# Two float32r parts in place of three bf16 parts in the last two mean passes

## What is computed

```
def _sage_layer(x, src, dst, W_l, b_l, W_r, gamma, beta):
    msg = x[src]
    summed = segment_sum(msg, dst);  cnt = segment_sum(1, dst)
    agg = summed / maximum(cnt, 1)[:, None]
    out = agg @ W_l.T + b_l + x @ W_r.T
    out = (out - mean(out)) * rsqrt(var(out) + 1e-5) * gamma + beta
    return relu(out)
x3 = sage(sage(x, layer 0), layer 1)
x  = layernorm(x + x3)
```

## Time and profile before

| | us |
|---|---|
| median of 3 runs | 1939.49 (1938.94 to 1941.75) |
| the profiled execution, its own time | 1941.41 |
| its span, first to last instruction | 1939.5 |

### The profile page before, as it was taken

One profiled execution on the slowest core, in us unless ns is written; L12 is line 12 of the kernel. 1 busy time (PEld: TensorE's weight loads), 2 busy tenths in 40 slices (PEclk: granted clock), 3 DMA queues, 4 the chain that ended last, 5 costly groups with the idle time before them and its releaser, 6 DMA issues. The chain is left out here.

```text
span 1939.5 us, 44470 instructions
## 1 busy us (share of the span) xinstructions
PE 1623.6 (84%) x13670; PEld 1310.2 (68%) x13670; DVE 1463.3 (75%) x4393; ACT 1049.4 (54%) x2866; POOL 937.0 (48%) x940
## 2 busy tenths in 40 slices
PE   6699999999999749998556988956588887499996
PEld 5588888888887616556455877856477777266664
DVE  5688888888887698996668888856888886644656
ACT  2577677776776366773306878830377785311000
POOL 4777777777776120000455777535667773200000
PEclk9799999999999859999755999976589998699998
DMA  6888788888887002333552111127121112254442
GB/s 197 251 268 244 243 261 245 258 264 259 260 247 238 11 5 80 126 126 126 161 111 53 42 41 42 36 62 193 40 59 40 42 41 86 86 194 173 171 170 91
DMA packets 148931, 273.61 MB, mean 141 GB/s; under 512 B 28039, under 2 KB 88909, under 8 KB 146436
## 3 DMA queue, kind: packets, MB, share of 16 engines
q1 hardware_dynamic: 110430, 192.44, 30.3%
q0 software_dynamic: 33408, 75.68, 14.6%
q10 hardware_dynamic: 4854, 2.55, 0.5%
HBM read 225.06 MB, written 45.51 MB: 140 GB/s over the span
## 5 line engine op out<-in xcount | busy, mean ns | idle before, releaser
L997 POOL DMA_INDIRECT gated_rows<-p_tab,src_idx x416 | 436.8, 1050 | 150.3 <-issue 124.9
L1405 POOL DMA_INDIRECT cur<-table,src_idx x240 | 245.3, 1022 | 105.9 <-issue 49.4
L2260 PE MATMUL bank<-counts,mean_xs 128*128 128x416 bf16 (+2 forms) x1350 | 220.4, 322 | 32.0 <-DVE mean_xs L1762 32.0
L1593 PE MATMUL bank<-attention_counts,h_sb 128*128 128x260 f32 (+1 forms) x900 | 216.4, 363 | 13.8 <-ACT attention_counts L1548 9.9
L1526 ACT ACTIVATE attention_lo<-attention_plain,w_left 128x128 fp32r<-128x128 bf16 x512 | 176.7, 394 | 87.1 <-DVE attention_plain L1640 87.0
L1038 PE MATMUL bank<-gated_wide_q,gated_comb 128*128 128x256 f32 x832 | 216.0, 382 | 0.0
L1114 ACT ACTIVATE gated_sig<-gated_pre 128x512 f32<-128x512 f32 x208 | 131.4, 632 | 152.9 <-DVE gated_pre L1202 145.6
L2260 PEld LDWEIGHTS bank<-counts,mean_xs 128*128 128x128 bf16 x1350 | 126.4, 98 | 116.8 <-issue 35.4
L1202 DVE TENSOR_TENSOR gated_pre<-bank,gated_rows 128x512 f32<-128x512 f32 x208 | 142.8, 687 | 79.3 <-PE bank L1038 79.3
L1576 PE MATMUL bank<-attention_wide_a,attention_lo 128*128 128x300 f32 x512 | 151.7, 380 | 46.0 <-issue 31.8
L1593 PEld LDWEIGHTS bank<-attention_counts,h_sb 128*128 128x128 f32 x900 | 146.8, 191 | 26.2 <-ACT attention_counts L1548 17.4
(11 more groups left out here) (450 smaller groups left out, 3983.2 us busy)
## 6 DMA issues: line engine op xcount, KB each, us to landing
counts<-count_tabs SPq DMA_DIRECT2D x16, 2675.0 KB, 9.8
h_sb<-in_edge_attr_dram SPq DMA_DIRECT2D x51, 512.0 KB
count_tabs<-mean_counts SPq DMA_DIRECT2D x40, 535.0 KB, 2.7
gated_relr<-rel_rows SPq DMA_DIRECT2D x104, 128.0 KB
gated_ids<-id_rows SPq DMA_DIRECT2D x26, 512.0 KB
gated_wide_q<-q_tab SPq DMA_DIRECT2D x208, 64.0 KB
attend_hot_lo<-low_hots SPq DMA_DIRECT2D x52, 256.0 KB
gated_ea<-in_edge_attr_dram SPq DMA_DIRECT2D x51, 256.0 KB
```

Of the source, the lines that this page charges most:

```text
L997: pool.indirect_dma_start(out=rows[:, q % TICKS, c, :], out_offset=None, in_=p_tab, in_offset=bass.IndirectOffsetOnAxis(ap=src_idx[:, b, j ...
L1405: pool.indirect_dma_start(out=ring_row(n, j), out_offset=None, in_=table, in_offset=bass.IndirectOffsetOnAxis(ap=src_idx[:, gathered_batch ...
L1593: mm = pe.matmul(BANKS_D[k % 2][:, 0:width], h_sb[:, m, :], counts[:, home(first), m, at:at + width], start=(m == 0), stop=(m == NT - 1), ...
L2260: mm = pe.matmul(BANKS_D[q % ND][:, 0:width], xs[l][:, m // 3, m % 3, :], counts[:, s % 2, m // 3, at:at + width], start=(m == 0), stop=(m ...
```

## The change

`xs` has two parts per value, in float32r: the value rounded to it, and what is left. A block has 50 matmuls. [...] ScalarE widens four of the five pieces with `copy`, VectorE the third one with `tensor_copy`. A piece waits until TensorE is through with the piece three before it. The next table is loaded when all pieces of the old one are widened.

The split is made by VectorE alone: a rounding copy (or, between the passes, a second relu with float32r output) and a subtraction. ScalarE's four casts per group or chunk are gone.

A block has 10 steps. The finish of a chunk is cut in three parts on VectorE: products, mean and variance one step after `products`; polynomial, scale, shift and what follows up to the second variance four steps after; the second polynomial and levelling nine steps after. ScalarE takes the roots three and eight steps after. A self product is multiplied two steps and taken three steps after its transposes. `products` of a block come at the fourth step of the next block (the second for the last ones).

To make room, buffers that are needed no more are freed before the passes (`early_sb`), and `counts` lies at the other end of the memory.

```diff
-            xs = [sb(f"xs{l}", [P, NT, 3, P], BF16) for l in range(2)]
+            xs = [sb(f"xs{l}", [P, NT, 2, P], F32R) for l in range(2)]
+            PIECE, SLOTS = 5, 3
+            wide = sb("wide", [P, SLOTS, PIECE, max(width for _, _, width, _ in M_BLOCKS)], F32R)
-            PARTS = 15
-            SELF = {PARTS * (g + 1): g for g in range(NG)}
-            FLIP, CROSS = 8, 4
+            PARTS = 10
+            NP = NT // PIECE
+            BY_ACT, BY_DVE, DVE_PIECE = NP - 1, 1, 2
+            PIECES, STEPS_ = 2 * LAST * NP, PARTS * LAST
+            SELF = {PARTS * g + 6: g for g in range(NG)}
+            SELF_LAG, TAKE_LAG = 2, 3
+            MEASURE_LAG, ROOT_LAG, SCALE_LAG, ROOT2_LAG, LEVEL_LAG = 1, 3, 4, 8, 9
+            FLIP = 3
+            FINAL = {l * STEPS_ + PARTS * (c + 1) + (3 if c < LAST - 2 else 1): (l, c) for l in range(2) for c in range(LAST - 1)}
+            FINAL[STEPS_ + 2] = 0, LAST - 1
+            FINAL[2 * STEPS_] = 1, LAST - 1
+            ALL_STEPS = 2 * STEPS_ + LEVEL_LAG + 1
+            def widen(i):
+                q, c = divmod(i, NP)
+                l, k = divmod(q, LAST)
+                s, (_, _, width, at) = min(k, NSB - 1), M_BLOCKS[k]
+                tiles = slice(c * PIECE, (c + 1) * PIECE)
+                return 16 * ((l * NSB + s) // 2 + 1), table_in[s % 2], wide[:, i % SLOTS, :, 0:width], counts[:, s % 2, tiles, at:at + width]
 # SP: loads of the tables
-                        sp.wait_ge(applied, (l + 1) * LAST if s == NSB - 1 else l * LAST + s + 1)
+                        blocks = (l + 1) * LAST if s == NSB - 1 else l * LAST + s + 1
+                        sp.wait_ge(widened_a, blocks * BY_ACT)
+                        sp.wait_ge(widened_d, blocks * BY_DVE)
 # ScalarE
+                    def widen_piece(i):
+                        landed, table, to, frm = widen(i)
+                        act.wait_ge(table, landed)
+                        reach(act, multiplied, i - SLOTS + 1)
+                        act.copy(to, frm).then_inc(widened_a, 1)
+                    for i in range(SLOTS - 1):
+                        widen_piece(i)
+                    for s in range(ALL_STEPS):
+                        l, n = divmod(s, STEPS_)
+                        if l < 2 and n in SELF:
+                            copy_self[l](act, SELF[n])
+                        if s - ROOT_LAG in FINAL:
+                            root(act, *FINAL[s - ROOT_LAG])
+                        if s - ROOT2_LAG in FINAL and FINAL[s - ROOT2_LAG][0] == 1:
+                            root2(act, 0, FINAL[s - ROOT2_LAG][1])
+                        i = s // 2 + SLOTS - 1
+                        if s % 2 == 0 and i < PIECES and by_act(i):
+                            widen_piece(i)
 # TensorE
-                            mm = pe.matmul(BANKS_D[q % ND][:, 0:width], xs[l][:, m // 3, m % 3, :], counts[:, s % 2, m // 3, at:at + width],
-                                           start=(m == 0), stop=(m == 3 * NT - 1), skip_group_check=True)
+                            if part == 0 and t % PIECE == 0:
+                                widened(pe, i)
+                            mm = pe.matmul(BANKS_D[q % ND][:, 0:width], xs[l][:, t, part, :], wide[:, i % SLOTS, t % PIECE, 0:width],
+                                           start=(m == 0), stop=(m == 2 * NT - 1), skip_group_check=True)
 # VectorE
+                    for g in range(NG):
+                        dve.tensor_copy(xs[0][:, cut(g), 0, :], x_sb[:, cut(g), :]).then_inc(rounded[0], 1)
+                        dve.wait_ge(rounded[0], g + 1)
+                        dve.tensor_tensor(xs[0][:, cut(g), 1, :], x_sb[:, cut(g), :], xs[0][:, cut(g), 0, :], ALU.subtract).then_inc(left_over[0], 1)
+                    def finish_due(s):
+                        if s % 2 == 0 and s // 2 + SLOTS - 1 < PIECES and not by_act(s // 2 + SLOTS - 1):
+                            widen_piece(s // 2 + SLOTS - 1)
+                        if s - LEVEL_LAG in FINAL and FINAL[s - LEVEL_LAG][0] == 1:
+                            level(*FINAL[s - LEVEL_LAG])
+                        if s - SCALE_LAG in FINAL:
+                            scale(*FINAL[s - SCALE_LAG])
+                        if s - MEASURE_LAG in FINAL:
+                            take_products(*FINAL[s - MEASURE_LAG])
```

More of the change, by code:

```diff
@@ L77, in sb, with early_sb @@
         return ctx.enter_context(nc.sbuf_tensor(name, shape, dt))
+    early = ExitStack()
+    def early_sb(name, shape, dt=F32):
+        return early.enter_context(nc.sbuf_tensor(name, shape, dt))
     def sem(name):
@@ L2290, in _ @@
                                 turn(l, SELF[n])
-                            if n - 1 in SELF:
-                                multiply_self[l](pe, SELF[n - 1])
-                            if final(l, n):
-                                products(*final(l, n))
-                            apply(l, n // PARTS, share(3 * NT, n % PARTS, PARTS))
+                            if n - SELF_LAG in SELF:
+                                multiply_self[l](pe, SELF[n - SELF_LAG])
+                            if l * STEPS_ + n in FINAL:
+                                products(*FINAL[l * STEPS_ + n])
+                            apply(l, n // PARTS, share(2 * NT, n % PARTS, PARTS))
                     products(1, LAST - 1)
@@ L2318, in add_dense, with widen_piece, take_products @@
                         dve.tensor_tensor(to, to, BANKS_D[q % ND][:, 0:width], ALU.add).then_inc(added, 1)
-                    def finish(p, c):
+                    def widen_piece(i):
+                        landed, table, to, frm = widen(i)
+                        dve.wait_ge(table, landed)
+                        reach(dve, multiplied, i - SLOTS + 1)
+                        dve.tensor_copy(to, frm).then_inc(widened_d, 1)
+                    def finish(p, c):
+                        take_products(p, c)
+                        scale(p, c)
+                        if p % 2 == 1:
+                            level(p, c)
+                    def take_products(p, c):
                         l, r, k, u = p % 2, p // 2, CHUNK[c], p * LAST + c
-                        n = k.stop - k.start
                         dve.wait_ge(self_taken[l], r * NG + -(-k.stop // GROUP))
@@ L2328, in finish, with scale @@
                         dve.wait_ge(summed, p * NT + k.stop)
-                        measure(dve, link, p, c)
+                        measure[0](dve, p, c)
+                    def scale(p, c):
+                        l, r, k = p % 2, p // 2, CHUNK[c]
+                        measure[1](dve, link, p, c)
                         dve.wait_ge(affine_in, 16 * 4)
@@ L2342, in finish @@
                             dve.wait_ge(joined, r * LAST + c + 1)
-                            measure2(dve, link, r, c)
-                            for t in range(k.start, k.stop):
-                                dve.tensor_scalar(z[:, t, :], z[:, t, :], mean2_of(t), rstd2_of(t), ALU.subtract, ALU.mult).then_inc(normed2, 1)
+                            measure2[0](dve, r, c)
                             return
@@ L2814, in build_program @@
         if l == 2:
-            counts = sb("counts", [P, 2, NT, M_COLS], BF16)
+            counts = ctx.enter_context(nc.sbuf_tensor("counts", [P, 2, NT, M_COLS], BF16, side="right"))
         settle_attention(l, a_s, a_d)
+    early.close()
     mean_passes()
```

141 lines of the change are left out of this document (65 added, 76 removed).

## The result

| | median us | lowest to highest | ratio to before |
|---|---|---|---|
| before, 4 runs | 1939.22 | 1936.48 to 1941.75 | |
| after, 4 runs | 1895.85 | 1890.21 to 1899.34 | 0.9776 (95%: 0.9755 to 0.9798) |

The change takes 43.4 us; 50.9 were forecast, so 1888.6, in a range of 1880 to 1905. The profiled execution of after took 1897.1 us (span 1895.2).

What follows compares the result with a forecast made beforehand. TensorE was taken to bound the wide blocks, VectorE's norm chain the end. Gains of 2.3 + 23.4 + 5.3 + 19.1 + 0.8 = 50.9 us from the median 1939.49 gave 1888.6 us; range 1880 to 1905.

Steps and rivals of the forecast that it cites:

- TensorE's block: Wide block on TensorE: 50 float32r matmuls at 0.180 us plus 2.1 us of other products, 11.1 us.
- the first pass: Six blocks at TensorE's 11.1 us plus 1.3 for VectorE finishing later: 67.9 against 91.27 us, gain 23.4.
- upper end of 0.227: Matmuls of 136 columns: 0.227 us each if two passes are needed, costing 7 us over both passes; 0.113 was taken.
- Rival C: float32r matmuls at 416 columns take two cycles per column, 19.5 us a block, 2000 us in all; chance 0.04.
- lateness with roots: In-order ScalarE gives a chunk's root 7.4 us into the block, though its variance is ready at 6.2.
- The choice between 2.26 and 1.24 us: VectorE's one wide piece per block: 2.26 us taken because source and destination runs differ, 1.24 by the contiguous-copy row.
- rival A: VectorE's piece runs at two elements per cycle: second pass -3.5 us, start -1.0, 1884 us in all; chance 0.25.
- VectorE's sum of 12.1 us per block: Second pass: chunk chain, accumulation, self product and widening on VectorE total 12.1 us per block, more than TensorE's 11.1.
- Start: Start to first accumulation: TensorE begins at 1675.0 after ScalarE's first piece; first accumulation at 1689.9, gain 2.3 us.
- Change of pass: Between the passes, narrow blocks set by VectorE: 25.6 against 30.91 us, gain 5.3, including 1.2 for the GpSimd memset.
- End: After the second pass, VectorE's chain: 10.0, 9.5, and 13.05 plus 0.5 us; 33.0 against 33.80, gain 0.8.
- the last 33 us as they were: Listed sign that the forecast is right: the kernel's closing stretch stays unchanged, about 33 us.

Runs made afterwards that it cites:

- experiment 5: Changed kernel with each chunk's finish made in one go one step after its products, both roots issued then: 1936.96 us, ratio 0.9981.
- experiment 2: Changed kernel with the ring's rows padded to 428, so a wide piece has five runs of 416 on both sides: 1897.83 us, ratio 0.9774.
- Experiment 1: Changed kernel with GpSimd's clearing of acc moved behind VectorE's splits of all groups: 1898.68 us, ratio 0.9777.
- experiment 8: Changed kernel with 14 (first pass) and 28 (second) further matmuls ahead of the eighth chunk's products, filling TensorE's wait: 1893.25 us, ratio 0.9766.
- experiment 6: Kernel before, keeping its bf16 parts, with only the chunk finish cut in three (scaling six, levelling thirteen steps after products): 1940.23 us, ratio 0.9995.
- e0_after: The changed kernel run again without an edit, beside the edited ones: 1900.43 us, ratio 0.9797.
- experiment 4: Changed kernel with all five pieces of a block widened by ScalarE, none by VectorE: 1889.85 us, ratio 0.9736.
- e10_scalar_late: Changed kernel with all pieces on ScalarE, acc cleared after the first splits, and the eighth chunk's products later in the first pass: 1888.63 us, ratio 0.9737.
- experiment 3: Changed kernel with the eighth chunk's products issued at step 4 (first pass) and step 8 (second) of the narrowest block: 1899.55 us, ratio 0.979.
- e9_together: Changed kernel with later acc clearing, ring rows padded to 428, narrow blocks' pieces on ScalarE, and later eighth-chunk products in the first pass: 1891.62 us, ratio 0.9755.

## Why the prediction was right, and where it was off

**TensorE's block.** Right in kind, small in size: the pitch at 416 columns is 0.193 us, where 0.180 was taken from the earlier trace rows. 50 x 0.193 = 9.65, and a full block of the first pass takes 11.45, so the other products are 1.8, not 2.1. That the first pass came out at 68.25 for 67.9 is partly luck. TensorE's share of it is 67.46, as experiment 5 shows, where every accumulation waits for TensorE, against 6 x 11.1 = 66.6. Six blocks at 11.45 would be 68.7, but the last takes 10.46, since the last group of the self product has one tile and not four. And VectorE was 68.25 - 67.46 = 0.8 us behind TensorE at the end of the pass, not 1.3. At 292 columns 35 matmuls took 5.0 us (change of pass), 0.14 each, for a forecast of 0.130. At 136, 45 took 5.2 us at full clock, 0.116 each, close to the 0.113 taken and far from the upper end of 0.227. Rival C is out by the first of these numbers.

**ScalarE.** 1929 ns for a forecast of 1.92 us. Its lateness with roots is there too (first pass, ScalarE and then VectorE):

```profile
1711.15 0.59 ACT L821 COPY mean_scratch<-bank 128x512 f32<-128x512 f32 x1 [0.33 <-PE bank L811]
1711.64 0.21 ACT L2120 ACTIVATE mean_n_root<-mean_n_var 128x3 f32<-128x3 f32 x1
...
1711.88 0.18 DVE L2111 RECIPROCAL mean_n_rstd<-mean_n_root 128x3 f32<-128x3 f32 x1 [1.91 <-ACT mean_n_root L2120]
```

The root stands right behind the self copy, 7.2 us after the accumulation at 1704.49 (forecast 7.4), and VectorE has the slack for the 1.91 us.

**VectorE.** The choice between 2.26 and 1.24 us was the prediction's main one, and 2312 ns decides it; experiment 2 shows that the shapes do it and not the type or the bf16 source, since with equal runs on both sides the same data take 1451. By the Trainium skill (VectorE: DVE Perf Modes, What auto-detection actually checks) two elements per cycle need outermost sizes that are both even or equal. The traces agree in the order: 2312 ns at five against one merged run, 1451 at five against five. But they do not show the full rate: the 0.52 ns per further element that the prediction took would give 1.24, so rival A's price was too low by 0.21 us, and the three pieces with equal runs (578, 1065 and 1451 ns for 680, 1460 and 2080 elements) lie 0.62 ns per further element apart. (The 0.52 and 1.04 ns in the prediction are such slopes too, not the time of a row divided by its elements: 688/1024 is 0.67 and 628/512 is 1.23.) Price aside, experiment 2, which is rival A made, gained 2.5 us in the second pass (forecast 3.5) and 0.8 in the start (forecast 1.0). VectorE's sum of 12.1 us per block was 0.3 too high for three of the blocks (11.82), and the first took 11.37 for 11.6, but two took 12.3 and 12.2. That gives the -0.8, of which 0.1 is arithmetic: 11.6 + 5 x 12.1 is 72.1, not 72.2.

**Start: the step that failed.** "First piece at 1672.9 + 1.92, TensorE starts at 1675.0" named ScalarE as the last to be ready, 2.1 us after its first piece begins; it was 3.9 us. TensorE waited for VectorE's first split (L2414), which the memset had held back for 2.6 us. I had charged the memset in the change of pass (1.36 us for one small operation) and not at the start, where it begins 0.04 us before the copy. Before the change ScalarE did that first cast. Experiment 1 gives 16.65 for the 17.1 forecast.

**Change of pass.** 25.6 forecast, 27.2 at full clock. The 25.6 are 26.9 from TensorE's end of the seventh block less the 1.3 by which VectorE was to be late. It was 0.8 late, and that is 0.5 of the 1.6. Counted from TensorE's end the three accumulations came at 9.4, 17.7 and 28.0, for 9.4, 17.3 and 26.9. The narrow pieces cost 1065 and 578 ns for 0.92 and 0.51, and the first block of the second pass carries 50 times the larger pitch (0.65 us): 0.9 of this 1.1. The 1.2 us charged for the memset did not come: it ran from 1779.52 to 1782.29, beside a piece that had begun before it, and the small operation at 1782.21 took 0.17 us. Nothing was saved by that, since the tenth accumulation waited 1.19 us for TensorE. What the prediction left out altogether is the clock: TensorE, not idle in the whole first pass, waits 2.12 us for VectorE there, and in other executions that costs about 4 to 6 us more.

**End.** 33.0 forecast, 35.1 measured: 10.57, 11.32 and 13.21 for 10.0, 9.5 and 13.55. The prediction counted VectorE's chain alone. TensorE, after

```profile
1871.18 1.17 PE L2312 MATMUL bank<-mean_w,acc 128*128 128x128 f32 x6 [4.04 <-DVE acc L2356]
1872.01 9.85 PE L2298 MATMUL bank<-mean_wide,mean_xs 128*128 128x136 f32 x45
```

took 0.22 us per matmul, and the last accumulation waited 2.02 us for it. In experiment 8, with the stretch before it filled, that wait is gone, the middle part takes 9.94 and the end 33.71; with the pieces on ScalarE too, 32.27. So 1.4 of the 2.1 are TensorE's clock, and the rest is VectorE's chain, priced about 0.5 too low for each of two chunks and 0.3 too high behind the last accumulation. The failed step is "the last 33 us as they were".

**Sum.** Start +2.2, change of pass +1.6, end +2.1, first pass +0.4, second -0.8, and 1.2 us of work ahead of the passes that is not the change's: +6.6 of the profiled execution's span. The stage ahead moves by itself: 1669.0 to 1675.9 over all the profiles here, though the kernels differ there only in where buffers lie; the two with the old places, before and experiment 6, have 1672.8 and 1673.3. The profiled execution was also a lucky one: it had the full clock in the change of pass, and `e0_after` took 4.3 us more there.

## What to carry to other kernels

When an engine is given work that another one needs every few microseconds, all that it waits for must be ready when its turn comes: the cut finish was worth nothing while TensorE set the pace and nearly all of the gain once ScalarE fed it. A faster TensorE begins to wait at the seams between stages, and a wait of 2 to 4 us can cost more afterwards, by the clock, than it lasts; add that to a forecast of any stage that changes from full to mixed, and try to fill such a wait. Price a new VectorE copy by a row with the same pair of shapes, and look at what GpSimd does at that moment.

## What was not expected of the hardware

- A GpSimd memset of 128x3200 beside a float32 rounding copy of 512 elements on VectorE, begun 0.04 us after it, made the copy take 3.00 us in place of 0.42: it ended 0.27 us after the memset. A two-element operation from SBUF to SBUF begun within another memset ended 0.02 us after it (1.36 us), while the operations on two tiles just before it ran their 0.3 to 0.6 us beside the same memset. A piece of 2080 elements kept its 2.31 us, but it began before the memset. Whether the kind of copy or the order makes the difference was not tried apart.
- The clock after a wait of 2.1 to 2.9 us in an otherwise full stretch is not the same from one execution to the next. Over the profiles of the changed kernel and its variants it fell to 1.2 GHz after six such waits (change of pass in `e0_after`, experiments 1, 2, 4 and `e10_scalar_late`; end of experiment 3) and not after four (change of pass in the first profile, experiments 3 and 5, `e9_together`). In experiment 5 it also fell after a wait of 1.5 us. It fell after none of up to 1.34 us, the filled ones among them, and after each of 3.3 us and more. What decides in between stays open.
- VectorE's conversion of bf16 to float32r with equal runs took 0.62 ns per further element (680, 1460 and 2080 elements), between the 0.52 and 1.04 of the prediction's slopes. The narrow pieces of the unedited changed kernel show it already, beside the wide ones with unequal runs.
